# Causal masks as pairs of 64-row products, and an expert's matmuls moved ahead of the value products, in a one-core attention and mixture-of-experts kernel

## The reference

```python
xn = layernorm(x)
qkv = xn @ wqkv.T                      # 16 heads of 64
q, k = rope(rmsnorm(q)), rope(rmsnorm(k))
attn = softmax(where(causal, q @ k.T * 64**-0.5, -inf))
a = (attn @ v) @ wo.T
e = argmax(xn @ gate_w.T)              # one of 8 experts per row
out = x + a + (xn + xn @ expert_w[e].T)
```

## Time and profile before

| | |
|---|---|
| median of 3 runs | 2049.13 us |
| runs | 2047.25 to 2049.21 us |
| profiled execution, span from first to last instruction | 2046.9 us |
| PE busy | 1980.4 us, 97% |
| DVE busy | 1742.6 us, 85% |
| ACT busy | 1601.8 us, 78% |
| POOL busy | 1374.5 us, 67% |
| mean granted TensorE clock | 0.993 |

### The profile page before, as it was taken

How to read it: one execution, slowest core, us unless ns; L and a number is a source line. 1 busy time by engine, 2 the same in 40 slices (tenths; PEclk the granted TensorE clock), 3 DMA queues, 4 the chain that set the end, 5 groups by cost and what they waited for, 6 DMA issues and landing times.

```text
span 2046.9 us, 46259 instructions
## 1 busy us (share of the span) xinstructions
PE 1980.4 (97%) x15496; PEld 1665.6 (81%) x15496; DVE 1742.6 (85%) x4144; ACT 1601.8 (78%) x5095; POOL 1374.5 (67%) x1968
## 2 busy tenths in 40 slices
PE   4899999999999999999999999999999999999997
PEld 4777888888888888888888888888888888888785
DVE  5899888888888888888988889889888888888875
ACT  3887887878788788787788878878878878878775
POOL 6667666577666777657766677656766677765764
PEclk8999999999999999999999999999999999999999
DMA  5110212112211132212121122221122112221244
GB/s 187 57 58 30 68 48 64 56 45 81 97 49 48 50 96 79 63 48 68 66 91 48 50 80 68 73 63 53 63 79 78 48 53 84 68 71 60 83 138 139
DMA packets 84540, 145.68 MB, mean 71 GB/s; under 512 B 9808, under 2 KB 63184, under 8 KB 84176
## 3 DMA queue, kind: packets, MB, share of 16 engines
q1 hardware_dynamic: 78160, 125.93, 19.2%
q0 software_dynamic: 6144, 16.79, 2.5%
HBM read 102.05 MB, written 40.63 MB: 70 GB/s over the span
## 4 chain that ended last, share of the span: by engine, by line
PE 86%; POOL 6%; DVE 4%; ACT 3%; issue 1%; DMA 0%; DVEq 0%; another core or an unknown queue 0%; POOLq 0%
PE ps_g L722 38%; PE ps_g L816 14%; PE ps_s L805 13%; PE ps_g L825 11%; PE ps_g L784 5%; PE ps_s L798 3%; POOL qk_rot L505 2%; POOL rms_inv L511 2%; ACT prob L603 2%; POOL qk_rot L516 2%; PE ps_g L749 1%; PE ps_g L731 1%; DVE qk_sin L995 1%; DVE qk_cos L995 1%; ACT qk_sq L587 1%
## 5 line engine op out<-in xcount | busy, mean ns | idle before, releaser
L505 POOL TENSOR_TENSOR qk_rot<-qk_cos,qk_sin 128x128 f32<-128x128 f32 x1024 | 466.6, 477 | 588.8 <-DVE qk_sin L995 579.5
L722 PE MATMUL ps_g<-w_qkv,xn_t 128*128 128x384 f32 (+1 forms) x3072 | 641.3, 351 | 2.3 <-DVE xn_t L910 1.5
L603 ACT ACTIVATE prob<-ps_s,neg_max 128x256 f32<-128x256 f32 (+3 forms) x1024 | 536.4, 551 | 0.3 <-DVE neg_max L1009 0.3
L722 PEld LDWEIGHTS ps_g<-w_qkv,xn_t 128*128 128x128 f32 x3072 | 525.9, 190 | 6.0 <-DVE k_t L1003 2.2
L511 POOL TENSOR_TENSOR rms_inv<-ss,neg_half 128x8 f32<-128x8 f32 x256 | 448.3, 1751 | 0.0
L1009 DVE TENSOR_REDUCE neg_max<-ps_s 128x2 f32<-128x512 f32 (+3 forms) x512 | 405.4, 811 | 0.0
L613 ACT ACTIVATE prob_t<-ps_g 128x512 f32<-128x512 f32 (+2 forms) x768 | 364.9, 526 | 43.7 <-PE ps_g L816 43.5
L816 PE MATMUL ps_g<-ident,prob 128*128 128x128 f32 x2560 | 355.6, 277 | 3.5 <-DVE prob L1020 1.6
L816 PEld LDWEIGHTS ps_g<-ident,prob 128*128 128x128 f32 x2560 | 290.5, 141 | 67.4 <-DVE prob L1020 43.8
L516 POOL TENSOR_TENSOR qk_rot<-qk_rot,rms_inv 128x256 f32<-128x256 f32 x512 | 324.2, 654 | 20.1
L805 PE MATMUL ps_s<-k_t,q_t 64*128 64x256 f32 (+3 forms) x3072 | 307.5, 332 | 0.0
(11 more groups left out here) (99 smaller groups left out, 2396.3 us busy)
## 6 DMA issues: line engine op xcount, KB each, us to landing
w_tile<-w_dram SPq DMA_DIRECT2D x120, 512.0 KB
x_rows_s<-x_dram SPq DMA_DIRECT2D x120, 128.0 KB, 2.7
y_dram<-y_rows_s SPq DMA_DIRECT2D x120, 128.0 KB
xin<-in_x SPq DMA_DIRECT2D x16, 512.0 KB, 4.2
out<-acc SPq DMA_DIRECT2D x15, 512.0 KB, 3.2
w_dram<-w_tile SPq DMA_DIRECT2D x8, 512.0 KB, 4.0
x_dram<-xn SPq DMA_DIRECT2D x2, 1920.0 KB, 18.1
y_back<-in_expert_t SPq DMA_DIRECT2D x8, 256.0 KB, 4.3
```

The lines of the kernel that those rows point to most:

```text
L505: r = pool.tensor_tensor(rot[:, :, a, :], cos[:, :, a, :], sin[:, :, 1 - a, :], ALU.add)
L603: r = act.activation(prob[:, h, prob_at(k):prob_at(k) + w], ps_s[n % 2][:, h, 0:w], ACT.Exp, bias=neg_max[:, i, h:h + 1], scale=1.0, accum ...
L722: r = pe.matmul(ps, lhs(a, c), rhs(b, c), start=(c == parts[0] and (a, b) == TERMS[0]), stop=(c == parts[-1] and (a, b) == TERMS[-1]))
```

## The change

Each 128-row mask matmul becomes two of 64 rows, one of 128 columns for the upper half of the diagonal tile and one of 64 columns for the lower half, with the two heads on different halves of the array. Two more constant tiles, built at the start, hold the swapped halves. On PE, the first expert (and a third tile's transposes) now come before the value products, which the second score visit follows directly. The order of bank uses follows, and ScalarE takes the value products' result after the expert's.

```diff
+        ident_x = sb("ident_x", [P, P], BF16)
+        mask_x = sb("mask_x", [P, P], BF16)
...
@@ uses(u)
+            found += [f"ex{i}" for i in tiles[0:1]] + [f"xs{i}" for i in tiles[2:3]]
             if live(u - 1):
                 found += ["o"]
-            found += [f"ex{i}" for i in tiles[0:1]] + [f"xs{i}" for i in tiles[2:3]]
...
@@ gpsimd, at the start
+            pool.memset(ident_x[:, :], 0.0)
+            pool.memset(mask_x[:, :], 0.0)
...
+            pool.affine_select(out=ident_x[:, 0:D], in_=ident_x[:, 0:D], compare_op=ALU.not_equal, fill=1.0,
+                               base=-D, pattern=[[-1, D]], channel_multiplier=1)
+            pool.affine_select(out=ident_x[:, D:P], in_=ident_x[:, D:P], compare_op=ALU.not_equal, fill=1.0,
+                               base=0, pattern=[[-1, D]], channel_multiplier=1)
+            pool.affine_select(out=mask_x[:, 0:D], in_=mask_x[:, 0:D], compare_op=ALU.is_ge, fill=MASKED,
+                               base=-D, pattern=[[-1, D]], channel_multiplier=1)
+            pool.affine_select(out=mask_x[:, D:P], in_=mask_x[:, D:P], compare_op=ALU.is_ge, fill=MASKED,
+                               base=0, pattern=[[-1, D]], channel_multiplier=1).then_inc(s_pool_self, 1)
+            pool.wait_ge(s_pool_self, seen(s_pool_self))
+            pool.affine_select(out=mask_x[:, D:P], in_=mask_x[:, D:P], compare_op=ALU.is_ge, fill=MASKED,
+                               base=D - 1, pattern=[[0, D]], channel_multiplier=-1)
...
@@ scalar unit(u)
-                if live(u - 1):
-                    take_o(u - 1)
...
                 for i in tiles[2:3]:
                     take_xs(u, i)
+                if live(u - 1):
+                    take_o(u - 1)
...
@@ tensor scores(u, k0)
-                for n in (n0, n0 + 1):
-                    i = ITEMS[n - NT * u]
-                    for h in range(HEADS_OF_PAIR):
-                        pe.matmul(ps_s[n % 2][:, h, tile(i)], ident_b[:, :], mask_b[:, :], start=True, stop=False,
-                                  skip_group_check=True)
+                for half in range(2):
+                    for n in (n0, n0 + 1):
+                        at = ITEMS[n - NT * u] * P
+                        for h in range(HEADS_OF_PAIR):
+                            ident_h, mask_h = (ident_b, mask_b) if h == half else (ident_x, mask_x)
+                            rows = slice(h * D, (h + 1) * D)
+                            pe.matmul(ps_s[n % 2][:, h, at + half * D:at + P], ident_h[rows, :], mask_h[rows, half * D:P],
+                                      start=(half == 0), stop=False, skip_group_check=True)
...
@@ tensor unit(u)
-                if live(u - 1):
-                    values(u - 1)
                 for i in tiles[0:1]:
                     expert(u, i)
                 for i in tiles[2:3]:
                     transpose_xs(u, i)
+                if live(u - 1):
+                    values(u - 1)
                 if live(u):
                     scores(u, 2)
```

## The result

The changed kernel takes 2072.59 us (median of 4 runs, 2072.12 to 2073.77) against 2048.19 us before on the same chip: ratio 1.012, 95% interval 1.0106 to 1.0135. It is 1.2% slower; its span is 2070.8 us.

What follows compares the result with a forecast made beforehand. PE's own sequence was taken as the bound, TensorE being busy 97% of the span. Terms +28.8 - 4.9 - 3.5 = +20.4 us on 2046.9 gave 2067.3; plus 2.2 for the median, 2069.5, called 2070; range 2055 to 2093.

Steps and rivals of the forecast that it cites:

- units without a tile: 19 of 128 units, PE order unchanged: both mask gains, 0.18 + 0.08 = 0.26 us each, were to count, -4.9 us.
- Part 1, the stall: At the expert, moved ahead of the value products: PE waits for VectorE's conversion of the expert's rows, standing 0.47 us.
- the lateness: VectorE's conversion ends 0.33 us after the value products' old start in most tile units, and again in each next unit.
- The expert and the value products: PE steps in the new order: expert 0.91 us including a shape change, value products 2.31 us as before.
- Part 2, the masks: Masks to scores 0.25 us instead of 0.33, scores 0.91 instead of 1.01; gain 0.18 in second visit, 0.08 in first.
- rival 1: The 64-row masks or their loads do not overlap: 0.33 us instead of 0.17, +24 us, some 2094; chance 0.12.
- the exposed load of the first score: Weight load of the first score behind a mask: taken as 0.10 us exposed, bounds 0.03 and 0.10.
- The sum for a tile unit: From the value products' old start to the projection: 4.46 us before, 4.75 after, +0.29; over all tile units +28.8 us.
- Given back at GpSimd: PE's 13 waits for GpSimd at the transposes of q and k, 5.1 us, shrink behind the stall: -3.5 us.
- What costs nothing: Later take_o on ScalarE and VectorE, rotated banks and GpSimd setup all hidden by idle time: no cost.
- Rival 2: At VectorE's conversion in tile units: no stall comes, fewer array-shape changes decide; 0.26 us gained a unit, 2016 us; chance 0.09.

Runs made afterwards that it cites:

- The runs with the extra instruction: One small VectorE fill added ahead of the conversion of the expert's rows: kernel before 2050.09 us (ratio 1.0), changed kernel 2081.53 us (1.0152).
- the run with the masks alone: Changed kernel with the new 64-row masks kept and the old order of expert and value products put back: 2035.01 us, ratio 0.9935.
- the one with the projection first: Changed kernel with the output projection moved between last qkv group and expert, VectorE's addition of it ahead of the probabilities' scaling: 2028.55 us; run again, 2029.13 us.
- the conversion made early: Changed kernel with VectorE's conversion between the first visit's row maxima, and the tile rows' transposes and ScalarE copy ahead of the last item's probabilities: 2032.99 us.
- the run with the masks of the second visit only: Old order of expert and value products, 64-row masks in the second visit, the 128-row masks of before in the first: 2042.50 us, ratio 0.9965.
- the same move: Next batch's row transposes ahead of the value products, projection between qkv and expert: 2040.08 us; with ScalarE and VectorE taking xn_t ahead of o_t too, 2017.75 us.

## Why the prediction was right, step by step

Forecast 2070, measured 2072.59; forecast +20.4 us on the span, measured 2070.8 - 2046.9 = +23.9. The 3.5 us between them are nearly all one term, the gain of the units without a tile, forecast 4.3 too large; the tile units' loss came out 0.8 below the forecast. The 2.2 us that the forecast added for what lies around the span set a median of runs against the span of one execution; for one and the same execution it is 1.8 (2072.57 against 2070.8).

- **Part 1, the stall.** Right in place, cause and size. Forecast from qkv to the expert: 1.24 + 0.37 = 1.61; measured 1.65. The 0.47 of standing appears as 0.35 in the list of waits, 97 times, because the profile counts the modelled end of the last matmul as busy (1089.71 + 1.30). The chain says that the lateness recurs in each unit for the reason given: the part ahead of the expert starts at the transposes of k less than a unit earlier (1081.85 against 1091.36). The runs with the extra instruction show it.
- **The expert and the value products.** Forecast 0.91 and 2.31; measured 0.89 and 2.31.
- **Part 2, the masks.** The 64-row masks do overlap (two starts at 1094.56), so rival 1 falls. From masks to scores 0.18 instead of 0.25, and the scores take 0.98 instead of 0.91: the exposed load of the first score stands in the scores, not ahead of them. The sum, 1.16, is the one forecast. The first score lasts 416 ns there against 333 for its neighbour, so 0.08 of the 0.10 is still exposed. The forecast also read 0.026 for a bf16 matmul of 64 columns out of a row whose eight matmuls have 64 to 8 columns; the one of 64 columns alone takes 0.032, which moves no term by more than 0.01. The visit that was mis-sized is the first: its 0.08 was to lie before the stall, and in a steady unit nearly all of it is lost to the transposes around it, as the run with the masks alone shows.
```profile
L823 PE MATMUL ps_s<-k_t,q_t x4: 333/374/416, 1094.7 to 1095.0; 64*128 64x384 f32 x4
```
- **The sum for a tile unit.** Forecast +0.29, measured 15.56 - 15.26 = +0.30 (the average of pair 3's units on both sides). Over all units with a tile, the periods add up to +24.5 us, against 28.8 - 3.5 = 25.3 forecast.
- **Given back at GpSimd.** Right: its 13 waits of 5.1 us are gone, and the units of pair 1, where such waits show, grew by 0.06 only, which over 13 units is about 3.1 us less than at pair 3's 0.30.
- **Units without a tile.** The term that was mis-sized: forecast -4.9 us, measured -0.6. The nine from the eleventh unit on gain 0.15 to 0.18 each, which is the second visit's 0.18; the first visit's 0.08 does not show in them. In one of them, the starts of the first visit's scores are 14.84 apart before (the first two rows below) and 14.69 after (the last two). The ten at the start, which I had counted alike, are together 0.95 longer. Of these, 1.02 stand in the very first unit, whose first scores start 0.7 earlier, while the wait for GpSimd at its transposes of q and k grows from 0.79 to 2.01 us. That is not shown to be the change's doing: two executions of one kernel, the one with the projection first, differ in the same way (1.09 and 2.00). What is shown is that the next nine gain 0.07 together instead of 2.3. PE waits for GpSimd there, 4.6 us (4 times) between 60 and 240 us before and 6.0 (7 times) after. I had taken a gain on PE as kept without asking what the transposes of q and k wait for next. The tile units' +24.5, these -0.6, and 0.7 less ahead of the first scores and 0.7 more behind the last unit's first scores make up the span's change.
```profile
471.71 1.30 PE L805 MATMUL ps_s<-k_t,q_t 64*128 64x256 f32 x12
486.55 1.31 PE L805 MATMUL ps_s<-k_t,q_t 64*128 64x256 f32 x12
475.25 1.07 PE L823 MATMUL ps_s<-k_t,q_t 64*128 64x256 f32 x10
...
489.94 1.29 PE L823 MATMUL ps_s<-k_t,q_t 64*128 64x256 f32 x12
```
- **What costs nothing.** take_o later on ScalarE, the banks and the setup show no wait of PE in the list, as forecast.
- **Rival 2** (faster, by fewer changes of array shape) describes what the change is worth once the stall is covered: with the conversion made early a tile unit took 15.04 us, with the projection as cover 14.9. The first is the better measure of the change alone; in the second the projection's own step is 0.11 shorter in its new place than in the changed kernel and the expert's 0.10, with 0.06 lost at the transposes of q and k. The rule of the Trainium skill, "TensorEngine Tiling (Array Packing)", Key Properties, that a change of mode drains the array, was not wrong here; it was outweighed. The trace agrees that a change costs time, though not by what: in the run with the masks alone, the expert's step to the masks takes 0.91 when they have another shape, against 0.82 before.

What stays open: in the run with the masks of the second visit only, that visit's masks, scores and expert save the full 0.08, but the steady unit is only 0.055 shorter; the other 0.03 is spread over small lengthenings of other groups, the largest 0.01 at the projection, and no run says why. And I did not try to remove what is left of the waits for GpSimd.

## What to carry to other kernels

An engine that is busy 97% of the time has cover in its order: before moving a consumer forward, read for each of its inputs not that it causes no wait today, but by how much it comes before, or behind, the place to which the consumer moves. If it comes behind, follow its queue back to the instruction that starts it; when that lies on the same engine's own path in the same period, the stall comes back every period and is worth its length times the number of periods. Then the remedy is to put other ready work over it, and to move the copies of that work in the other engines' queues along with it: the same move was worth 11 us less or 11 us more than leaving it out (2017.75 against 2029.13, 2040.08 against 2028.55), by that alone.

## What the runs showed of the hardware

- **64-row bf16 matmuls on the two halves of the array start together**, 0.06 to 0.07 us from one pair of 128 columns to the next; the eight masks and the step to the scores take 0.18 us where four of 128 rows and a change of array shape took 0.33.
- **A VectorE instruction can cost half of its shown length**: the fill of 0.165 us moved the end of the instruction behind it by 0.08.
- **A GpSimd rotation that starts during a long VectorE addition of two operands in the on-chip memory ends only after it.** In the run with the projection first, the pair of L520 takes 0.87 us in most units and 1.86 in the unit in which VectorE adds 128x1024 elements (L935) at the same time, and the next transposes of q and k wait 0.67 us for GpSimd. In the kernel before it is the same for all 16 such additions: the rotation that starts 0.24 to 0.25 us into the addition lasts 1.44 instead of 0.46 and ends 0.31 to 0.32 after the addition's end. These additions fall into the units of pair 1, the ones that wait for GpSimd in the earlier trace rows, and there the last rotation ends 1.1 us later in the unit than in pair 3. I did not try to move the addition. That it is the two engines' access to that memory is likely, not shown.
```profile
1041.08 1.86 POOL L520 TENSOR_TENSOR qk_rot<-qk_cos,qk_sin 128x128 f32<-128x128 f32 x2 [0.90 <-DVE qk_sin L1013]
...
1056.71 0.87 POOL L520 TENSOR_TENSOR qk_rot<-qk_cos,qk_sin 128x128 f32<-128x128 f32 x2 [0.93 <-DVE qk_sin L1013]
```
```profile
1041.25 1.38 DVE L935 TENSOR_TENSOR acc<-xin,xn 128x1024 f32<-128x1024 f32 x1
```
